# The second batch's normalized tiles: from a transpose out of DRAM to a plain load and a transpose out of SBUF

## The reference

```python
def attn(x):                       # x is normalized first
    q, k, v = x @ wq.T + bq, x @ wk.T + bk, x @ wv.T + bv      # each cut into 16 heads
    probs = softmax(where(causal, -inf, q @ k.T / 8))
    return (probs @ v) @ wo.T + bo
x = x + layernorm(attn(layernorm(x)))
x = x + layernorm(ffn(layernorm(x)))
```

## Time and profile before

| | before |
|---|---|
| median of three runs | 2567.19 us |
| the profiled execution | 2570.42 us, its span 2568.4 us |
| PE busy | 2317.3 us (90%) |
| DVE, ACT, POOL busy | 1793.0, 1712.2, 1837.3 us (70, 67, 72%) |
| DMA queue of the program | 445.57 MB, 95.2% of 16 engines |
| `pt<-hl` transposes (line 300) | 768, 4.6 us from issue to landing |
| `arena<-xn_scratch` transposes (line 285) | 16, 5.6 us |
| granted TensorE clock, mean | 0.969 |

### The profile page before, as it was taken

The page is one execution under the profiler, slowest core; times in us unless marked ns, Lnnn a source line. Parts: engine busy times, 40 slices in busy tenths (PEclk is TensorE's granted clock), DMA queues, the critical chain, the costliest instruction groups (busy, mean ns, idle before and its releaser), DMA issues. The chain is left out here.

```text
span 2568.4 us, 72133 instructions
## 1 busy us (share of the span) xinstructions
PE 2317.3 (90%) x28626; PEld 1453.9 (57%) x28626; DVE 1793.0 (70%) x4218; ACT 1712.2 (67%) x2451; POOL 1837.3 (72%) x1551
## 2 busy tenths in 40 slices
PE   4899999999999998889999999999996559999995
PEld 2556666565757655556575757566664335444442
DVE  8577877677777655556666766666665637888886
ACT  3477777777877766567777777777777834444443
POOL 4477888788888867678888888888887734555553
PEclk9999999999999999999999999999998779999997
DMA  9599999999999999989999999999999866666663
GB/s 236 124 186 181 200 195 191 195 195 186 199 190 198 177 186 188 193 154 182 175 180 179 171 189 175 187 164 182 173 166 198 172 142 142 151 158 160 153 149 89
DMA packets 1433646, 450.17 MB, mean 175 GB/s; under 512 B 1410240, under 2 KB 1411536, under 8 KB 1433312
## 3 DMA queue, kind: packets, MB, share of 16 engines
q1 hardware_dynamic: 1433312, 445.57, 95.2%
HBM read 67.95 MB, written 41.94 MB: 43 GB/s over the span
## 5 line engine op out<-in xcount | busy, mean ns | idle before, releaser
L815 POOL TENSOR_TENSOR hl<-probs,hl 128x1024 f16<-128x1024 f32 (+7 forms) x768 | 1231.8, 1615 | 395.7 <-ACT hl L696 394.2
L690 ACT ACTIVATE probs<-s_ps,exp_bias 128x1024 f32<-128x1024 f32 (+7 forms) x768 | 655.7, 854 | 410.3 <-DVE exp_bias L541 406.3
L538 DVE TENSOR_REDUCE neg_max<-s_ps 128x1 f32<-128x1024 f32 (+7 forms) x768 | 694.6, 904 | 66.5 <-PE s_ps L396 66.1
L696 ACT ACTIVATE hl<-probs 128x1024 f16<-128x1024 f32 (+7 forms) x768 | 620.5, 808 | 48.1 <-DMA pt<-hl 24.1
L414 PE MATMUL o_ps<-v,pt 128*128 128x65 f16 x4352 | 453.6, 194 | 84.5 <-DMA pt<-hl 75.0
L396 PE MATMUL s_ps<-nat 64*128 64x512 f16 (+3 forms) x3840 | 434.6, 355 | 69.3 <-ACT probs L690 64.9
L414 PEld LDWEIGHTS o_ps<-v,pt 128*128 128x128 f16 x4352 | 404.5, 97 | 136.3 <-DMA pt<-hl 64.2
L415 PE MATMUL o_ps<-v,pt 128*128 128x65 f16 x4352 | 453.5, 195 | 0.0
L416 PE MATMUL o_ps<-v,pt 128*128 128x65 f16 x4352 | 451.5, 193 | 0.0
L443 PE MATMUL u_ps<-arena,w 128*128 128x512 f16 x1008 | 389.7, 387 | 40.2 <-DMA arena<-hl 35.2
L415 PEld LDWEIGHTS o_ps<-v,pt 128*128 128x128 f16 x4352 | 404.3, 98 | 27.0
(11 more groups left out here) (148 smaller groups left out, 3791.8 us busy)
## 6 DMA issues: line engine op xcount, KB each, us to landing
w_raw<-in_w_pairs SPq DMA_DIRECT2D x48, 576.0 KB, 4.7
o_scratch<-o_hl SPq DMA_DIRECT2D x128, 128.0 KB, 2.5
out<-result SPq DMA_DIRECT2D x32, 512.0 KB, 3.6
x_in<-in_x SPq DMA_DIRECT2D x27, 512.0 KB, 4.6
pt<-hl SPq DMA_TRANSPOSE x768, 4.6
nat<-in_x SPq DMA_DIRECT2D x16, 512.0 KB, 4.5
xn_scratch<-xn SPq DMA_DIRECT2D x16, 512.0 KB, 4.7
xn<-in_x SPq DMA_DIRECT2D x11, 512.0 KB, 4.0
```

Source lines behind the costliest of these rows:

```text
L538: nc.vector.tensor_reduce(neg_max[:, r, acc, h:h + 1], s_ps[n % S_RING][:, 0:nb * P], AX_X, ALU.max, negate=True).then_inc(max_done, 1)
L690: nc.scalar.activation(probs[n % P_RING][:, 0:nb * P], s_ps[n % S_RING][:, 0:nb * P], ACT.Exp, bias=exp_bias[:, r, acc, h:h + 1], scale=SO ...
L696: nc.scalar.activation(hl[n % HL_RING][:, 0:nb * P], probs[n % P_RING][:, 0:nb * P], ACT.Copy).then_inc(p_hi_done, 1)
L815: nc.gpsimd.tensor_tensor(hl[n % HL_RING][:, w:2 * w], probs[n % P_RING][:, 0:w], hi, ALU.subtract).then_inc(p_lo_done, 1)
```

## The change

The 16 tiles no longer come transposed out of DRAM. Each is first loaded plainly (512 KB, contiguous rows) from `xn_scratch` to one of two buffers, `x_in` seen as float16 or `xn`, in turn, and is then transposed from there into `xt`. `TURN_AT` gives the steps of the transposes, counted from the start of pair 6: 10, 12, 14, 15, 17, 19, 21, 22, 24, 26, 28, 29, 31, 33, 35, 36, so that the last one is at step 12 of pair 7, and not at 16. The load of a tile (`FETCH_STEPS`) is issued at the step of the transpose before it, behind that transpose and ahead of the step's `pt` transposes; the first load is at step 8 of pair 6.

SP's waits: a transpose waits for its load (`fetched`) in place of `xn_stored`; the first two loads wait until all tiles are stored and split, each later load for the landing of the transpose that read its buffer, the one before the last.

```diff
-TURN_STEPS = {"pre": {10 + 2 * i: i for i in range(7)}, "turn": {2 * i: 7 + i for i in range(9)}}
+
+TURN_AT = [7 * (n // 4 * 4) // 4 + (10, 12, 14, 15)[n % 4] for n in range(LN_TILES)]
+TURN_STEPS = {divmod(NSTEP * (HALF_PAIRS - 2) + at, NSTEP): n for n, at in enumerate(TURN_AT)}
+FETCH_STEPS = {divmod(NSTEP * (HALF_PAIRS - 2) + at, NSTEP): n for n, at in enumerate([8] + TURN_AT[:-1])}
...
+        fetched = [sem(f"fetched{i}") for i in range(2)]
...
+        back = [x_in[:].bitcast(F16), xn[:]]
...
             def body(p, kind):
                 for i in range(NSTEP):
-                    n = TURN_STEPS.get(kind, {}).get(i)
+                    n = TURN_STEPS.get((p, i))
                     if n is not None:
                         tile = TURN_TILES[n]
-                        sp.wait_ge(xn_stored, 16 * (tile + 1))
+                        sp.wait_ge(fetched[n % 2], 16 * (n // 2 + 1))
                         sp.wait_ge(unit_done, units_before(HALF_PAIRS - 1, [(m, tile // 4) for m in "qkv"]))
-                        transpose_x(LN_TILES + n, tile, xn_scratch[tile])
+                        transpose_x(LN_TILES + n, tile, back[n % 2])
+                    n = FETCH_STEPS.get((p, i))
+                    if n is not None:
+                        if n < 2:
+                            sp.wait_ge(xn_lo_done, 2 * LN_TILES)
+                            sp.wait_ge(xn_stored, 16 * LN_TILES)
+                        else:
+                            sp.wait_ge(xt_done[(n - 2) % 4], 16 * ((LN_TILES + n - 2) // 4 + 1))
+                        sp.dma_start(back[n % 2], xn_scratch[TURN_TILES[n]]).then_inc(fetched[n % 2], 16)
```

## The result

The changed kernel is slower: ratio 1.0083 to the kernel before, 95% interval 1.0071 to 1.0096, that is +21 us (+18 to +25); the medians of ten runs each are 2592.64 and 2567.98 us, 24.7 apart; below I go by the ratio. I had forecast +10, 2577 us, with a range up to 2593. The sign and the place were right; the forecast was half of what came, and the median lies at the very end of the range.

What follows compares the result with a forecast made beforehand. TensorE paces undisturbed pairs; transfers or their issue pace the first stretch (26 steps from step 10 of pair 6). First stretch +24, second -14, together +10 us: 2580 profiled, 2577 median, range 2559 to 2593.

Steps and rivals of the forecast that it cites:

- What bounds the stretch: 26 steps from step 10 of pair 6: transfers or their issue set the pace, 2.1 us for each 512 KB transpose.
- Source of the transposes, taken as 0: All 16 transposes: reading SBUF instead of DRAM changes each by between -0.6 and +0.6 us, taken as 0.
- 16 loads at 2 us, 32 in all, of which 20 were to remain: SP's queue, first stretch: each unabsorbed load costs about 2 us; SP's waits, falling from 24.5 to 11 us, absorb part.
- My sign for the slower issue: SP's queue: the pt transpose issued behind a load takes near 3.5 us, against 1.78 behind nothing.
- Two more transposes in the first stretch, 4 us: Two of the last three transposes move before step 12 of pair 7, costing 2 x 2.1 = 4 us.
- New waits of SP, up to 4 us: SP waits for a load before its transpose: up to 1 us at four tiles with one step between, otherwise 0.
- Rival 2: First stretch: SP's waits for its loads decide, about 2 us for each of 16 tiles; +24 in all, 2591; chance 0.14.
- Second stretch, -14: Step 12 of pair 7 to the next store: loses the step-18 wait and other waits, 12.4 us, -14 with small waits.
- small waits: Second stretch: unspecified short waits that go, taking the 12.4 us saving to 14.
- Rival 1 (the loads hide): First stretch: SP's waiting and free DMA time absorb the loads; -11 to +1 in all, some 2562; chance 0.23.
- Rival 3 (transposes at the plain rate): First stretch: SBUF transposes move at 434 GB/s, 15 taking 18 us instead of 36; -8 in all, 2559; chance 0.02.
- Rival 4 (the dense schedule gains less): Second stretch: the step-18 wait moves elsewhere, -8 instead of -14, 2583; counted inside the forecast's 0.54.

Runs made afterwards that it cites:

- the run with five buffers: The steps alone with a pt ring of 5 buffers instead of 4 and an hl ring of 5 instead of 6; ratio 0.9878 to the kernel before, -31 us.
- the steps alone: Kernel before with only the new transpose steps: transposes still read DRAM, no loads; ratio 0.9976 to the kernel before, -6 us.
- the late loads: Changed kernel with each load issued behind its step's two pt transposes instead of ahead of them; ratio 1.0077 to the kernel before, +20 us.
- 4 KB loads: The steps alone plus 16 loads that nobody reads, each 32 bytes of each row; ratio 1.0006 to the kernel before.

## Why the prediction came out as it did

- **What bounds the stretch**: right. More was moved per microsecond (209 to 212 GB/s against 187 to 188) and TensorE waited more for `pt`, 26.8 and 28.0 us. (One reading was off: PE stands at 9 tenths from slice 3 to 30; slice 31 reads 6.) My sum has no term for TensorE's own work, though PE was busy 6 to 8 us longer at the lower granted clock; whether that is part of the price or only follows from the waits, no run shows.
- **Source of the transposes, taken as 0**: right by two runs, -1.5 us by the times and +0.3 in the trace. The difference in rate, 218 against 291 GB/s, was measured where each ran alone and doesn't show in the full stretch; why not was only argued (a slower start of the DRAM reads). My sign against the mechanism, transposes from SBUF that land clearly sooner than 5.6 us, came out mixed in the changed kernel, 4.7 us in the median from `x_in` and 5.8 from `xn`; with the same steps and no loads it is 5.5 us from either source, so it isn't the source.
- **16 loads at 2 us, 32 in all, of which 20 were to remain**: this is the term that was mis-sized. The runs say 29 us by the times, and 25 in the stretch, where only 15 of the loads are: 0.5 each whatever the size, and 1.1 to 1.3 more for 512 KB. The price per load was nearly right; the discount for SP's reserve wasn't. I let SP's waits fall from 24.5 to 11 us and so pay 13 us; the 11 came from setting the DMA engines' share to 88%, for which no row speaks. They stayed: 24.0 and 25.8 us, and with the loads alone added it went from 27.2 to 31.6. That the first stretch still came out at 178.6 and 181.0 against my 178 is luck, two errors that cancel. SP's time without these waits rose by 25 us (178.6 - 24.0 against 129.4) and not by 38, and its waits not at all. My sign for the slower issue, near 3.5 us for the `pt` transpose behind a load, came 6 times of 16; the other ten took 1.2 to 1.9 us. So SP's waits for TensorE were no reserve here. That they belong to a loop in which each of the two waits for the other in turn is my reading of the lists of waits, where both stand; no run shows it by itself, and the run with five buffers can't settle it.
- **Two more transposes in the first stretch, 4 us**: 3 us in the steps alone. Right without loads, 7.5 us together with their loads.
- **New waits of SP, up to 4 us**: none seen. Rival 2 falls, and the late loads show what it would have been.
- **Second stretch, -14**: -11 in both traces, -9 in the steps alone. The wait at step 18 went, as the prediction said. Over-counted were 3 us. The "small waits", 1.6 us, had no row; which part of the rest was too much isn't shown.
- **Ahead of the first transpose**: I gave it nothing, though the first load lies there: 37.4 us in both traces against 35.7 and 35.0, about 2.
- **The sum**: +25 - 11 + 2 = +17 in the traces where I had +24 - 14 = +10, and 21 by the times. The missing 4 are the scatter or the part outside that stays open. +21 is just beyond the +20 that I gave the forecast itself. The upper end of the range, 2593, was drawn for rival 2, whose waits didn't come, and that 2592.64 still lies below it is luck.
- **Rival 1 (the loads hide)**: falls; even 4 KB loads cost 8 us. **Rival 3 (transposes at the plain rate)**: falls, by rows 8 and because the source made no difference. **Rival 4 (the dense schedule gains less)** came true in part: 9 to 11 us in the second stretch, a net gain of 6 without loads and of at most 4 with them.

## What to carry to other kernels

In this stretch, which transfers pace, an added 512 KB transfer cost about its full time on the DMA engines (1.1 to 1.3 us) and 0.5 us beside it, though the issuing queue showed 24.5 us of waiting. Before such waits are counted as reserve, ask whether the engine that the queue waits for itself waits for that queue's transfers, as TensorE did here: then they may not shrink at all. A detour through SBUF has to save more than its own load, and here the source of a transpose saved nothing. Of a change with two ideas try each alone: the denser schedule gave 6 us, the loads took 29.

## What I had not expected

- A transpose of 512 KB alone on the DMA engines moves 291 GB/s out of DRAM and 218 out of SBUF (readings of 1.0 and 1.5 us), and yet both take the same in a full stretch (157.51 and 157.80 us for 26 steps).
- 16 transfers of 4 KB cost 7.8 us in the trace and 8, give or take 6, in the times: in a full queue a tiny transfer has nearly a third of the price of one of 512 KB.
- One more `pt` buffer for one less `hl` buffer takes 25 us (1%) off the kernel and nothing off the stretch that waits most for `pt`.
